# Attention loop of a graph network: repeated mask products on TensorE, an earlier bias product and reordered hand-overs

## The reference, cut to what matters

```python
q = (x @ Wq.T).reshape(N, H, C); k = ...; v = ...       # N=12500, H=8, C=16
edge_bias = edge_attr @ We.T                            # 200000 x 8
scores = einsum('ehc,ehc->eh', q[dst], k[src]) / sqrt(C) + edge_bias
seg_max = segment_max(scores, dst, num_segments=N)
ex = exp(scores - seg_max[dst])
denom = segment_sum(ex, dst, num_segments=N)
out = segment_sum(v[src] * (ex / denom[dst])[:, :, None], dst, num_segments=N)
```

## Time and profile before

| | |
|---|---|
| median of three timed runs | 6654.04 us |
| the profiled execution, its own time | 6652.28 us |
| its span in the trace | 6650.5 us |
| mean granted TensorE clock | 0.753 of full speed |
| busy: PE, DVE, ACT, POOL | 81%, 66%, 34%, 47% |

### The profile page before, as it was taken

How to read it: one execution, slowest core, us unless ns; L and a number is a source line. 1 busy time by engine, 2 the same in 40 slices (tenths; PEclk the granted TensorE clock), 3 DMA queues, 4 the chain that set the end, 5 groups by cost and what they waited for, 6 DMA issues and landing times. The chain is left out here.

```text
span 6650.5 us, 159851 instructions
## 1 busy us (share of the span) xinstructions
PE 5406.7 (81%) x49582; PEld 3559.8 (54%) x49582; DVE 4418.8 (66%) x13500; ACT 2281.1 (34%) x5686; POOL 3152.5 (47%) x3144
## 2 busy tenths in 40 slices
PE   4587777878887788875599699998899997699995
PEld 2354444545454445554477466665466665466664
DVE  7455555555555555558799677776477776677776
ACT  3222222222222222223344233333533333433332
POOL 2455555555555555555200055553255553455552
PEclk9655555555555555555677699999999999899997
DMA  4433333333333333333333433333433333533335
GB/s 140 122 92 89 91 89 89 91 90 93 90 91 88 89 92 91 92 88 109 112 95 91 120 107 106 103 104 96 134 106 107 103 103 98 169 103 104 106 104 152
DMA packets 541998, 688.37 MB, mean 104 GB/s; under 512 B 217072, under 2 KB 427905, under 8 KB 541722
## 3 DMA queue, kind: packets, MB, share of 16 engines
q0 software_dynamic: 140208, 338.71, 18.3%
q1 hardware_dynamic: 401692, 348.45, 17.4%
HBM read 619.25 MB, written 67.52 MB: 103 GB/s over the span
## 5 line engine op out<-in xcount | busy, mean ns | idle before, releaser
L744 POOL DMA_INDIRECT at_kv<-kv_tab,at_idx x1568 | 1605.2, 1024 | 1169.3 <-issue 491.3
L2254 ACT ACTIVATE ag_msg<-ag_pair 128x768 bf16<-128x768 f32 x1200 | 927.9, 809 | 1582.9 <-PE ag_pair L2184 1114.8
L2193 PE MATMUL ag_sum<-ag_hot,ag_msg 128*128 128x240 bf16 x10800 | 1307.2, 268 | 91.9 <-issue 73.8
L2193 PEld LDWEIGHTS ag_sum<-ag_hot,ag_msg 128*128 128x128 bf16 x10800 | 973.5, 98 | 473.8 <-issue 395.6
L2068 POOL DMA_INDIRECT ag_spill<-g_tab,ag_idx x600 | 584.6, 974 | 1224.1 <-DMA ag_idx<-spill_tab 578.9
L2123 DVE CAST ag_msg<-ag_pair 128x768 bf16<-128x768 f32 x600 | 573.2, 955 | 582.0 <-PE ag_pair L2184 267.2
L2075 POOL DMA_INDIRECT ag_spill<-g_tab,ag_idx x750 | 726.9, 969 | 460.9 <-issue 178.1
L2184 PE MATMUL ag_pair<-xs,ag_pick 128*32 128x384 bf16 x14400 | 809.4, 331 | 135.2 <-issue 83.1
L2106 DVE TENSOR_SCALAR ag_hot<-iota_win,ag_node 128x240 bf16<-128x240 bf16 x4350 | 902.5, 290 | 1.5 <-PE ag_sum L2193 1.5
L2184 PEld LDWEIGHTS ag_pair<-xs,ag_pick 128*32 128x32 bf16 x14400 | 304.7, 95 | 447.7 <-issue 282.7
L799 DVE TENSOR_REDUCE at_ml<-at_ps_bc 128x4 f32<-128x512 f32 x392 | 252.8, 686 | 362.0 <-PE at_ps_bc L999 229.8
(11 more groups left out here) (330 smaller groups left out, 8859.7 us busy)
## 6 DMA issues: line engine op xcount, KB each, us to landing
ag_pick<-slot_tab SPq DMA_DIRECT2D x150, 768.0 KB
rk_hi_bc<-hi_tab SPq DMA_DIRECT2D x50, 896.0 KB
at_attr<-attr SPq DMA_DIRECT2D x196, 128.0 KB
at_qd<-q_tab SPq DMA_DIRECT2D x1568, 12.0 KB
at_kv<-kv_tab,at_idx POOLq DMA_INDIRECT x1568
ag_spill<-g_tab,ag_idx POOLq DMA_INDIRECT x1350
tr_dv<-dinv_tab SPq DMA_DIRECT2D x72, 256.0 KB
g_tab<-xs SPq DMA_DIRECT2D x48, 384.0 KB
```

The costliest lines, as they stand in the source:

```text
L744: nc.gpsimd.indirect_dma_start(kv[:, s.slot, ch, :], None, env["kv_tab"], bass.IndirectOffsetOnAxis(ap=idx[:, s.slot, ch:ch + 1], axis=0)) ...
L2193: last = nc.tensor.matmul(sum_ps[k][:, 0:WIN], row[:, part * DIM:(part + 1) * DIM], hot[:, k, ch, :], start=first and part == 0, stop=end ...
L2254: nc.scalar.activation(msg[:, p % 4, :, :], pair_ps[p % 3][:, :, 0:3 * DIM], ACT.Copy).then_inc(copied[p], 1)
```

## The change

Six edits of `attend`:

1. The pair `mask(0)`, `mask(1)` is issued six times a round on TensorE where it was issued once. Each repetition starts the accumulation anew and writes the same values into the same banks; `spread_scores` adds to the last.
2. `bias` goes from behind `spread_q` to a place ahead of `turn_near`, and its wait for `scaled` goes away: the result of `spread_scale` (`sf_ps`) moves out of the bank `ps_scale`, which `bias` writes, into the bank `ps_node`. `num_ps` moves by 16 columns and `den_ps` onto columns of the node sums.
3. `add_bias` goes ahead of `shrink` and `raise_max` on VectorE, `turn_scores` ahead of `spread_q` and `turn_max` on TensorE, `copy_scores` ahead of `scale_exp` and `copy_max` on ScalarE.
4. `give_back` goes behind `spread_scores`, `fall_short` from the end of a round to the next round (lag 4) behind `run_max`, with a second copy of `ml` for it, and `gain_exp` to the front of ScalarE's list at lag 4. `run_max` waits for `short_made` of two blocks back.
5. `spread_scale` waits for `nodes_made` and `count_copied` instead of the next block's `above_made`, and `shrink` for `placed` instead of `scale_spread`. `node_max` goes ahead of `scale_nodes`.
6. `pace`: the fourth gather waits for `nodes_made` (four blocks back) instead of `near_read`, the seventh for `hot_made` of this block instead of `added`.

```diff
-        ml = tile("ml", [P, HEADS])
+        ml = tile("ml", [P, 2, HEADS])
...
-        sf_ps = ps_scale[:, 0:128]
+        sf_ps = ps_node[:, 144:272]
...
-        num_ps, den_ps = ps_node[:, 256:384], ps_node[AUXD:AUXROWS, 384:512]
+        num_ps, den_ps = ps_node[:, 272:400], ps_node[AUXD:AUXROWS, 0:128]
...
                     if ch == 3:
-                        s.freed(pool, near_read, 3)
+                        s.freed(pool, nodes_made, 4)
...
-                    if ch == 6 and not (isinstance(s.n, int) and s.n < 4):
-                        pool.wait_ge(added, 2 * (s.nth - 4))
+                    if ch == 6:
+                        pool.wait_ge(hot_made, s.nth)
...
-                        s.freed(dve, short_made, 1)
+                        s.freed(dve, short_made, 2)
...
                 def shrink(s):
-                    dve.wait_ge(scale_spread, s.nth)
+                    dve.wait_ge(placed, s.nth)
...
-                    (3, run_max(0)), (3, run_max(1)), (3, own_max), (2, products), (3, above_score),
-                    (4, scale_nodes), (4, load_bases), (3, node_max), (2, add_up), (3, load_first), (4, shrink),
-                    (3, raise_max), (2, add_bias), (4, merge), (0, place_one), (0, hot_one),
-                    (3, messages), (3, fall_short)], w)
+                    (3, run_max(0)), (3, run_max(1)), (4, fall_short), (3, own_max), (2, products), (3, above_score),
+                    (3, node_max), (4, scale_nodes), (4, load_bases), (2, add_up), (2, add_bias), (4, shrink),
+                    (3, load_first), (3, raise_max), (4, merge), (0, place_one), (0, hot_one), (3, messages)], w)
...
                 def spread_scale(s):
                     pe.wait_ge(scale_made, s.nth)
-                    pe.wait_ge(above_made, s.nth if isinstance(s.n, int) and s.n == sh.BLOCKS - 1 else s.nth + 1)
+                    pe.wait_ge(nodes_made, s.nth)
+                    pe.wait_ge(count_copied, s.nth)
...
                     s.freed(pe, above_made, 1)
-                    if not (isinstance(s.n, int) and s.n < 2):
-                        pe.wait_ge(scaled, 2 * (s.nth - 2))
...
-                    (2, mask(0)), (2, mask(1)), (3, spread_max), (3, near_max), (4, spread_scale), (4, put_nodes),
-                    (3, turn_near), (1, spread_q), (2, bias), (3, turn_max), (2, turn_scores), (3, give_back),
-                    (2, spread_scores), (0, turn_hot), (0, turn_place), (3, sum_up)], w)
+                    (2, mask(0)), (2, mask(1)), (3, spread_max), (3, near_max), (2, mask(0)), (2, mask(1)), (2, bias),
+                    (3, turn_near), (2, mask(0)), (2, mask(1)), (4, spread_scale), (4, put_nodes), (2, mask(0)),
+                    (2, mask(1)), (2, turn_scores), (2, mask(0)), (2, mask(1)), (1, spread_q), (2, mask(0)), (2, mask(1)), (3, turn_max),
+                    (2, spread_scores), (3, give_back), (0, turn_hot), (0, turn_place), (3, sum_up)], w)
...
-                    (3, exp), (4, copy_count), (3, scale_exp), (3, copy_max), (2, copy_scores), (0, cast_place),
-                    (3, gain_exp), (0, copy_hot), (0, copy_place), (0, widen_hot)], w)
+                    (4, gain_exp), (3, exp), (4, copy_count), (2, copy_scores), (3, scale_exp), (3, copy_max),
+                    (0, cast_place), (0, copy_hot), (0, copy_place), (0, widen_hot)], w)
```

More of the change, by code:

```diff
@@ L797, in run @@
                         dve.wait_ge(bc_made[j], s.nth)
-                        s.freed(dve, short_made, 1)
-                        nc.vector.tensor_reduce(ml[:, HALF * j:HALF * (j + 1)],
+                        s.freed(dve, short_made, 2)
+                        nc.vector.tensor_reduce(ml[:, s.slot % 2, HALF * j:HALF * (j + 1)],
                                                 ps_bc[j][:, :].rearrange("p (h e) -> p h e", e=P), AX.X, ALU.max
@@ L807, in own_max @@
                     s.freed(dve, near_made, 1)
-                    nc.vector.tensor_tensor(md[:, :, :], ml[:, :].unsqueeze(1).to_broadcast([P, C, HEADS]),
+                    nc.vector.tensor_tensor(md[:, :, :], ml[:, s.slot % 2, :].unsqueeze(1).to_broadcast([P, C, HEADS]),
                                             env["mask_c"][:, :].unsqueeze(2).to_broadcast([P, C, HEADS]), ALU.mult
@@ L856, in fall_short @@
                     s.freed(dve, less_made, 1)
-                    nc.vector.tensor_tensor(short[:, :], back_ps, ml[:, :], ALU.subtract).then_inc(short_made, 1)
+                    nc.vector.tensor_tensor(short[:, :], back_ps, ml[:, s.slot % 2, :], ALU.subtract).then_inc(short_made, 1)
                 def scale_nodes(s):
```

## The result

The changed kernel takes 6920.78 us (median of 4, 6918.67 to 6932.51), the kernel before 6654.84 (4 runs): a ratio of 1.0394 (1.0379 to 1.0410). The forecast of 6176 us and its range are missed, on the other side of no change.

What follows compares the result with a forecast made beforehand. No engine was full; a ring of hand-overs between VectorE and TensorE bound the round. GpSimd's 10.3 us plus 1.4 lateness gave 11.7 instead of 14.14 us, times 195 rounds saving 476 us: 6176 us, range 5930 to 6600.

Steps and rivals of the forecast that it cites:

- The lateness: TensorE results usable later than modelled ends, 2.7 us a round before; half, 1.4, was charged after the change.
- GpSimd's floor: Eight gathers a round take 10.3 us; rival with no lateness: 10.3 to 10.5 us a round, 5921 us, chance 0.16.
- The clock: Repeated full-width bf16 mask products would lift TensorE's granted clock in the attention loop from 0.56 to at least 0.85.
- First half: Round from run_max to add_bias: 5.6 us instead of 10.33, the 1.75 us wait before add_bias falling under 0.4.
- VectorE's busy time: Sign in the attention loop: VectorE's work would stay at 8.26 us a round.
- `shrink` behind `placed`: Second half of the round: shrink's new wait for placed could cost 0 to 0.9 us if its cover is short.
- the sign that the prediction named: Over 0.5 us idle before shrink, released by put_nodes, would put the new wait for placed on the path.
- Ten repeats: Ten more mask products on TensorE: 2.2 us a round at 2.4 GHz, 4.2 at 1.2 GHz.
- The slower rival: Clock doesn't rise, TensorE becomes the bound at 15.5 us a round: 6925 us, chance 0.14; clock under 0.65.
- Wrong above all if lateness is not tied to the clock: Main stated risk: lateness was halved because TensorE's products would run at nearly twice the clock.

Runs made afterwards that it cites:

- Reorder only: Changed kernel without its ten repeated mask products: 5629.99 us (0.980) where the kernel before takes 5755.15, 6810.23 us (1.023) where it takes 6653.76.
- e12: Changed kernel with 16-byte SyncE transfers put between bias and add_bias and between put_nodes and shrink: 6945.45 us, 1.043 of before.
- narrow ones: Changed kernel with each of the ten repeats cut from 512 to 32 columns: 5658.84 us (0.984) on one chip, 6753.47 us (1.015) on another.
- e4: Changed kernel with each of the five repeated mask pairs issued twice, twenty repeats: 5855.90 us, 1.018 of before.
- repeats only: Kernel before plus ten repeated mask products in its own order: 5620.08 us (0.977) where before takes 5755.15, 6700.73 us (1.007) where it takes 6653.76.
- four repeats: Changed kernel with repeated pairs ahead of spread_scale and turn_max only, instead of ten repeats: 5618.86 us, 0.975 of before.

## Why the prediction was wrong

- *The lateness, 1.4 us a round: the step that failed.* I bounded it by 0 and its value of before, 2.7, and tied it to TensorE's clock. It hangs on the gathers, whose number the change leaves alone, and today's value was no upper bound. With 2.7 instead of 1.4 the sum would still have said 13.0 us; what was measured is 15.58, 5.3 us above the 10.3 of GpSimd's floor that the sum started from.
- *The clock, at least 0.85.* 0.73 on the record, 0.98 on a prompt chip. Right for a TensorE that runs on (1.00 and 0.99 on late chips with one and four gathers, from 500 to 1500 us); late results stop it, as in the round above. Reorder only and the changed kernel have TensorE busy for the same share on prompt chips, 932.01 and 933.91 of 1000 us, at clocks of 0.67 and 0.98, so the repeats do raise it. The prediction's reading of its rows was loose, though. From 4000 to 4500 us, at 1.00, about half of the products (2964 of 6028) use 32 of the array's 128 columns, and the stretch at 0.75 is nearly all bf16 products on the full array, so those two stretches don't show the kind of product to be what matters. The Trainium skill (TensorE: Matmul & The Clock Gate, "Why this matters for your kernels") puts a fall down to idle gaps between bursts. This case differs: from 500 to 1500 us the longest idle time of TensorE is 0.67 us in reorder only and 0.90 in the changed kernel, and the first has a mean clock of 0.67 all the same.
- *First half: the wait of `add_bias`.* Forecast under 0.4 us a round, measured 0.15. VectorE's busy time, forecast 8.26, is 8.30 (1278.70 by 154). Both right.
- *`shrink` behind `placed`, 0 to 0.9 us.* 1.0 on a prompt chip, hidden under GpSimd's floor; 3.0 on the record. It is the sign that the prediction named, idle time of over 0.5 us with `put_nodes` as releaser. By e12 it looks like a place and not a cause, which is not shown.
- *Ten repeats, 2.2 us at the full clock, hidden.* Hidden on prompt chips. On late ones all ten cost 0.64 us a round in the changed order (15.58 against 14.94) and 0.31 in before's; against narrow ones their columns cost 0.87.
- *GpSimd's floor, 10.3.* 10.26 to 10.29 in five kernels on prompt chips: the best number of the prediction. The rival of that name was the result there. On the record GpSimd's share of the loop fell from 58% to 49%, where it was to rise to 70%.
- *The slower rival, 15.5 us and 6925 us.* Its numbers fit the record within 0.5%, its reason does not: the clock was 0.73 and not under 0.65, and TensorE was busy 12.5 us of a round (1931.94 by 154), not all of it. TensorE as the bound is what e4 shows, at twenty repeats. That the sizes agree is chance.
- *"Wrong above all if lateness is not tied to the clock"*: so it was. On late chips the kernel before with one gather has 2% at a clock of 0.68, repeats only with all eight have 35% at 0.82. Their stretches, 500 to 2000 us:

```profile
500.00:2000.00 1500.00, 1348.48 (x9102) 850.63 (x9103) 1129.93 (x2896) 545.47 (x2208) 131.64 (x138) 0.68 0.14 33
```

```profile
500.00:2000.00 1500.00, 1190.34 (x7874) 643.06 (x7870) 856.54 (x2170) 408.03 (x1658) 851.99 (x829) 0.82 0.32 89
```

What stays open: why some chips are late and others are not; by which path a gather holds up TensorE's counts and SyncE's transfers; and why the changed order suffers more under it than that of before. Denser gathers are not the reason: three or more in 4 us are 34% of the changed kernel's time and 42% of before's. The same density leaves more results late in the new order (84% against 58%). None of its edits was tried by itself, the new waits of the fourth and seventh gather (edit 6) among them. Of the complete kernels that ran on a late chip none beats the kernel before; on a prompt one, four repeats (5618.86) and ten (5623.72) are alike.

## What to carry to other kernels

A wait with the releaser "remote" behind a short product is a cost with a cause of its own; until the cause is known, its upper bound isn't today's value, and a gain from closing gaps should not be charged against it at half. Ask first what else the chip does in those microseconds (here eight indirect transfers a round), since a kernel with few of them may behave in another way altogether. And a change that gains 2.4% on one chip lost 4% on another: where a tuned kernel runs near the rate of its gathers, compare on more than one chip before the order of hand-overs is blamed.

## What the runs showed of the hardware

- The same program takes 5755 and 5762 us on two chips and 6652 to 6657 on three others and in the record, 15.6% more. Of the 895 us between the profiles of before (6650.5 and 5755.2 us of span), 621 are in the attention loop. The rest is nearly all behind it, where gathers run as well; what it is due to was not tried.
- On late chips results of TensorE become usable up to 6 us behind their recorded ends, and then several nearly at once. In the round of reorder only shown above the last product of `sum_up` ended at 1408.43 and was counted at 1414.74, and two later products were counted within 0.12 us after it; so `above_score` waited until 1414.83 and `node_max` started at 1414.97. With one gather a round there is none of it in the changed kernel and 2% in that of before; the record's lengths of gathers (958 ns mean on the record, 974 on a prompt chip) don't show the difference.
- On a late chip gathers of 512-byte rows do as much harm as gathers of 1024-byte rows: 15.50 and 15.58 us a round.
